# Perceiver block on one core: cross attention with its probabilities normalised before they are turned

## The chip, the cores and the metric

One Trainium2 chip, of which the program uses 1 core. The time is that of one execution on the device, in microseconds, as the median of several runs. The profile is one further execution of the same program, recorded by the hardware profiler, with a time and a span of its own. TensorE does the matrix products, VectorE and ScalarE the work on their results in PSUM, GpSimd elementwise work in SBUF; SyncE issues the loads.

## The reference, cut to what matters

The block is a cross attention, a differential attention over heads with its feed-forward, and a layer of experts. Only the first is touched:

```python
def _L0_xattn_ref(x_q, x_k, x_v, W_Q, b_Q, ...):     # x_q (8, 64, 512), x_k = x_v (8, 1601, 512)
    Q = (x_q @ W_Q + b_Q).reshape(B, L, H, dk).transpose(0, 2, 1, 3)    # H = 16, dk = 32
    K = (x_k @ W_K + b_K).reshape(B, S, H, dk).transpose(0, 2, 1, 3)
    V = (x_v @ W_V + b_V).reshape(B, S, H, dk).transpose(0, 2, 1, 3)
    scores = jnp.einsum('bhld,bhsd->bhls', Q, K) / jnp.sqrt(jnp.float32(dk))
    attn = jax.nn.softmax(scores, axis=-1)
    ctx = jnp.einsum('bhls,bhsd->bhld', attn, V)
    ...
x = x + _L0_xattn_ref(_layernorm(x, axis=-1), ctx_1024, ctx_1024, ...)
```

## The kernel before

Everything is float32. Where a product must be exact to float32, each operand is split into a high part in the format fp32r and the rest (`_hi`, `_lo`), and `mm3` (L62) makes three matmuls of a pair.

The cross attention (L233) runs over 8 batches and, in each, two halves h of the heads: 16 units. A unit has 8 heads; two heads share a 128-row tile (their 64 queries each), so there are 4 tiles p of probabilities `prob[:, p]`, 128 x 1601, in two pair groups g. The four engines each have their own written-out order, `unit(b, h, last)`, and meet by semaphores:

- TensorE (L446): seven `values` steps (two 128-row tiles of the context each, V into PSUM), with eight `scores` steps put behind them by `STEPS_BEHIND` (L294): steps 0 to 3 are group 0, 4 to 7 group 1. Then, for each g, seven `turn` steps (transpose of two column tiles of both probabilities of the group), each followed by parts of the keys of the next unit (`HALVES_AT`) and by `weigh` of the step before (probabilities times values). Behind turn 2 of each group stands `sums` (L395): two matmuls of `ones` with a diagonal of inverse row sums, which lay the inverses out along the free axis. `select` (L437) gathers the group's output.
- VectorE (L604): low parts of values, keys and turned probabilities; `scores` copies scores from PSUM to `prob` and takes their maxima; `sums(b, h, g)` (L574) is the reciprocal of two row sums; `output` (L594) multiplies the four blocks of a group with the laid-out inverses `rsb`.
- ScalarE (L516): high parts; `exponentials` (L492) of a whole 128 x 1601 tile in place, with its row sum, for p = 0, 1 behind values 3 and 4 and for p = 2, 3 behind turns 1 and 3 of group 0; `inverses` (L498) writes the diagonals; `sums` (L511) copies the result to `rsb`.
- GpSimd (L321): for each batch and each of 4 chunks of 402 columns of the turned context, the high part by a multiplication with ones (L331) and the low part by a subtraction (L334). For all but the first batch it first waits for TensorE to have finished with the old chunk.
- SyncE (L297): context chunks into two buffers `craw`, each load behind the `c_lo` of the chunk two before (L306), and the queries `qbd`, each behind the scores of a whole unit (L310). These stand in one queue.

In the unit of the trace that is used below (batch 3, h = 0), the values begin at 422.8 us and the first turn at 447.65 us. Inside a unit, the wait of a first turn is this:

```python
                if t == 0:
                    pe.wait_ge(exp_done, b * 8 + (4 * h + 2 * g + 2))
```

## Time and profile before

| | us |
|---|---|
| median of 3 runs (1821.58 to 1823.15) | 1822.5 |
| profiled execution, its time | 1819.43 |
| its span | 1817.6 |
| TensorE busy in the span (matmuls) | 1425.5 |
| VectorE, GpSimd, ScalarE busy | 958.4, 654.7, 612.2 |

About 1.8 us of the execution lie outside of the span. Busy time is summed over the whole program; the cross attention takes about 63 to 975 us of the span, its 16 units 56.14 us each from the second on (the last is shorter, as it has no keys to make). In timelines and in stretches, all times count from the start of the span, and a bracket at the end of a line is the idle time before it with what ended that.

### The profile page before, as it was taken

To read this page: it belongs to the slowest core of one execution; us is meant where nothing else is said; L and a number is where in the kernel's file an instruction comes from. 1 tells how busy PE (TensorE), PEld (TensorE's weight loads), DVE (VectorE), ACT (ScalarE), POOL (GpSimd) and SP (SyncE) were. 2 spreads that over 40 slices of the span, in tenths; PEclk is the share of its full clock that TensorE was granted. 3 is DMA by queue.
4 is the path that set the end of the run, shared out by engine and by line. 5 is a ranking of instruction groups with operands and counts; after the bars stand their busy time and mean duration, and the time that the engine had idled before them with its cause. 6 is when DMAs were issued, how large, how long until landed. Compare 5 with 4: busy or idle time off the path is not lost. (4 is left out here: it accounts for less than half of the span.)

```text
span 1817.6 us, 23549 instructions
## 1 busy us (share of the span) xinstructions
PE 1425.5 (78%) x8688; PEld 1217.8 (67%) x8688; DVE 958.4 (53%) x2159; ACT 612.2 (34%) x1230; POOL 654.7 (36%) x260
## 2 busy tenths in 40 slices
PE   3599999999999999999996630112389565999995
PEld 2599999999999999999995420001267453555552
DVE  7155545555555555555554598995601553444443
ACT  4144344443445434454434232112321201232231
POOL 4505023050220502205003599895652312344442
PEclk8799999999999999999998765555689686999997
DMA  3401002010020200201003000000500209999999
GB/s 140 167 7 61 25 1 79 7 62 24 1 79 7 79 7 1 80 7 43 1 1 117 35 0 0 0 1 0 191 1 0 99 1 361 336 333 337 342 331 304
DMA packets 42619, 166.70 MB, mean 92 GB/s; under 512 B 5792, under 2 KB 6304, under 8 KB 33952
## 3 DMA queue, kind: packets, MB, share of 16 engines
q1 hardware_dynamic: 32352, 141.32, 21.2%
q0 software_dynamic: 10176, 24.12, 5.3%
q8 instruction: 62, 1.02, 0.2%
q14 instruction: 29, 0.24, 0.0%
HBM read 144.98 MB, written 20.45 MB: 91 GB/s over the span
## 5 line engine op out<-in xcount | busy, mean ns | idle before, releaser
L331 POOL TENSOR_TENSOR c_hi<-craw,ones 128x1608 fp32r<-128x1608 f32 x32 | 91.9, 2871 | 621.8 <-PE ps_x L66 548.1
L64 PE MATMUL ps_x<-wkv_hi,c_hi 128*128 128x256 f32 (+1 forms) x832 | 240.3, 289 | 0.0
L65 PE MATMUL ps_x<-wkv_lo,c_hi 128*128 128x256 f32 (+1 forms) x832 | 233.4, 281 | 0.0
L66 PE MATMUL ps_x<-wkv_hi,c_lo 128*128 128x256 f32 (+1 forms) x832 | 232.8, 280 | 0.0
L64 PE MATMUL ps_x<-c_hi,wkv_hi 128*128 128x402 f32 x512 | 196.2, 383 | 34.0 <-POOL c_lo L334 34.0
L583 DVE TENSOR_TENSOR pT<-ps_x,pT 128x512 fp32r<-128x512 f32 (+1 forms) x224 | 145.6, 651 | 125.9 <-ACT pT L508 122.7
L65 PE MATMUL ps_x<-c_lo,wkv_hi 128*128 128x402 f32 x512 | 178.0, 348 | 0.0
L66 PE MATMUL ps_x<-c_hi,wkv_lo 128*128 128x402 f32 x512 | 177.5, 347 | 0.0
L508 ACT CAST pT<-ps_x 128x512 fp32r<-128x512 f32 (+1 forms) x224 | 124.6, 557 | 140.2 <-PE ps_x L418 136.6
L553 DVE TENSOR_TENSOR vv<-ps_x,vv 128x512 fp32r<-128x512 f32 (+1 forms) x112 | 73.0, 652 | 176.7 <-ACT vv L489 176.7
L64 PEld LDWEIGHTS ps_x<-wkv_hi,c_hi 128*128 128x128 f32 (+1 forms) x832 | 153.2, 184 | 16.9 <-issue 16.9
L489 ACT CAST vv<-ps_x 128x512 fp32r<-128x512 f32 (+1 forms) x112 | 62.3, 556 | 288.1 <-PE ps_x L66 288.1
L1772 PE MATMUL ps_e<-e_w_gu,e_xT 128*128 128x512 f32 x344 | 157.5, 601 | 0.0
L547 DVE SCALAR_TENSOR_TENSOR kT_lo<-ps_x,bk,kT_hi 128x402 fp32r<-128x402 f32 x128 | 81.4, 636 | 140.8 <-ACT kT_hi L483 140.8
L65 PEld LDWEIGHTS ps_x<-wkv_lo,c_hi 128*128 128x128 f32 (+1 forms) x832 | 153.5, 184 | 0.0
L66 PEld LDWEIGHTS ps_x<-wkv_hi,c_lo 128*128 128x128 f32 (+1 forms) x832 | 153.3, 184 | 0.0
L1077 PE MATMUL ps_h<-ident,h_on 128*128 128x128 f32 x16 | 4.4, 432 | 178.8 <-POOL h_on L833 178.8
L433 PE MATMUL ps_x<-pT,vv 128*128 128x256 f32 (+1 forms) x832 | 135.1, 285 | 2.5 <-DVE pT L583 2.5
L566 DVE TENSOR_SCALAR_CACHE_REDUCE prob<-ps_x 128x402 f32<-128x402 f32 (+1 forms) x256 | 131.2, 569 | 0.0
L433 PEld LDWEIGHTS ps_x<-pT,vv 128*128 128x128 f32 (+1 forms) x832 | 124.8, 188 | 5.3 <-DVE pT L583 3.9
L418 PE MATMUL ps_x<-ident,prob 128*128 128x128 f32 (+1 forms) x832 | 127.0, 272 | 0.0
L1077 PEld LDWEIGHTS ps_h<-ident,h_on 128*128 128x128 f32 x16 | 2.9, 217 | 180.8 <-issue 99.0
(290 smaller groups left out, 3232.2 us busy)
## 6 DMA issues: line engine op xcount, KB each, us to landing
e_w_gu<-w_gu SPq DMA_DIRECT2D x49, 1024.0 KB, 8.1
craw<-ctxT SPq DMA_DIRECT2D x32, 804.0 KB, 4.5
e_w_dn<-w_dn SPq DMA_DIRECT2D x48, 512.0 KB, 5.6
f_raw<-slabs SPq DMA_DIRECT2D x8, 1024.0 KB, 4.8
h_raw<-slabs SPq DMA_DIRECT2D x5, 1024.0 KB, 4.9
qbd_dram<-qbd_all SPq DMA_DIRECT2D x2, 2048.0 KB, 6.9
qbd<-qbd_dram SPq DMA_DIRECT2D x16, 256.0 KB, 2.7
wraw<-w_qkv SPq DMA_DIRECT2D x3, 1024.0 KB, 8.4
```

The lines of the kernel that those rows point to most:

```text
L64: nc.tensor.matmul(out, a_hi, b_hi, start=start, stop=False)
L65: nc.tensor.matmul(out, a_hi, b_lo, start=False, stop=False)
L66: return nc.tensor.matmul(out, a_lo, b_hi, start=False, stop=stop)
L331: nc.gpsimd.tensor_tensor(c_hi[:, :, chunk(c)], craw[:, c % 2], ones[:, 0:1].unsqueeze(2).to_broadcast([P, KD, CW]), ALU.mult).then_inc(sp ...
L418: ins = nc.tensor.transpose(ps[0:r, 6 + n % 2, c:c + P], prob[:, 2 * g + j, P * st:P * st + r], ident[:])
L433: ins = nc.tensor.matmul(ps[:, 4 + g, 256 * j:256 * j + 256], vv[0:r, st, 2 * g + j].rearrange("p l c -> p (l c)"), pT[0:r, n % 2, st % 2, ...
L508: nc.scalar.copy(pT[0:r, n % 2, 0:w, :, 0].rearrange("p a j c -> p (a j) c"), ps[0:r, 6 + n % 2, 0:256 * w].rearrange("p (a c) -> p a c", ...
L547: nc.vector.scalar_tensor_tensor(kT_lo[:, m, chunk(c)], ps[:, n % KEY_BANKS, 0:CW], bk[:, 2 * h + m:2 * h + m + 1], f32(kT_hi[:, m, chunk( ...
L553: nc.vector.tensor_tensor(vv[0:r, 2 * v:2 * v + w, :, 1].rearrange("p a j c -> p (a j) c"), ps[0:r, V_BANK[v], 0:256 * w].rearrange("p (a ...
L566: ins = nc.vector.tensor_scalar(prob[:, p, CW * n:CW * n + w], ps[:, 2 * (i % 2) + j, 0:w], 0.0, None, ALU.add, ALU.max, accum_out=pmax[:, ...
L583: nc.vector.tensor_tensor(pT[0:r, n % 2, 0:w, :, 1].rearrange("p a j c -> p (a j) c"), ps[0:r, 6 + n % 2, 0:256 * w].rearrange("p (a c) -> ...
L1772: ins = nc.tensor.matmul(ps[:, GU], xT[:, b, P * g:P * g + P], w_gu[:, b, g], start=(g == 0), stop=(g == KD - 1))
```

## The change

The inverse of a row sum is applied by GpSimd to the whole tile `prob[:, p]` in SBUF, in place, before the tile is turned. The diagonals, the matmuls that lay them out, `rsb` and its copy are gone; `output` is a plain copy. The first turn of a group waits for both multiplications instead of both exponentials. VectorE takes the reciprocals one by one. The exponentials of p = 2, 3 stand one turn earlier. The high part of the context is made by ScalarE (`context`), put among the values of the units with h = 1, and GpSimd keeps the subtraction.

```diff
         def _(pool):
-            freed_by = (2, 4, 5, NV)
...
-                    pool.wait_ge(c_loaded[c % 2], b * 32 + 16 * (c // 2 + 1))
-                    nc.gpsimd.tensor_tensor(c_hi[:, :, chunk(c)], craw[:, c % 2], ones[...], ALU.mult).then_inc(split_hi, 1)
...
+            def split(b, c):
+                pool.wait_ge(split_hi, b * 4 + (c + 1))
+                nc.gpsimd.tensor_tensor(c_lo[:, :, chunk(c)], craw[:, c % 2], f32(c_hi[:, :, chunk(c)]),
+                                        ALU.subtract).then_inc(split_done, 1)
+
+            def normalise(b, h, p):
+                pool.wait_ge(inv_done, b * 8 + (4 * h + p + 1))
+                nc.gpsimd.tensor_scalar(prob[:, p, 0:S], prob[:, p, 0:S], rinv[:, p:p + 1], None, ALU.mult).then_inc(normed, 1)
...
         def _(pe):
             def scores(b, h, i):
-                elif i == 1:
-                    if b or h:
-                        pe.wait_ge(rsb_done, b * 4 + 2 * h)
...
-            def sums(b, h, g):
-                if g == 0:
-                    pe.wait_ge(sc_kept, b * 16 + (8 * h + 8))
-                else:
-                    pe.wait_ge(rsb_done, b * 4 + (2 * h + 1))
-                pe.wait_ge(diag_done, b * 8 + (4 * h + 2 * g + 2))
-                for j in range(2):
-                    ins = nc.tensor.matmul(ps[:, 3, ...], ones[:], diag[:, g, j], start=True, stop=True)
...
             def turn(b, h, g, t):
                 if t == 0:
-                    pe.wait_ge(exp_done, b * 8 + (4 * h + 2 * g + 2))
+                    pe.wait_ge(normed, b * 8 + (4 * h + 2 * g + 2))
...
         def _(act):
-            def inverses(b, h, g):
-                act.wait_ge(inv_done, b * 4 + (2 * h + g + 1))
-                for j in range(2):
-                    nc.scalar.activation(diag[:, g, j], ident[:], ACT.Copy, scale=rinv[...]).then_inc(diag_done, 1)
...
-            def sums(b, h, g):
-                act.wait_ge(sums_full, b * 4 + (2 * h + g + 1))
-                act.wait_ge(o_done, b * 4 + (2 * h + g + 1))
-                nc.scalar.copy(rsb[:, g], ps[:, 3, 256 * g:256 * g + 256]).then_inc(rsb_done, 1)
+            def context(b, c):
+                act.wait_ge(c_loaded[c % 2], b * 32 + 16 * (c // 2 + 1))
+                nc.scalar.copy(c_hi[:, :, chunk(c)], craw[:, c % 2]).then_inc(split_hi, 1)
...
             def unit(b, h, last):
                 for v in range(NV):
                     values(b, h, v)
+                    if h == 1 and not last and v in (2, 4, 6):
+                        context(b + 1, v // 2 - 1)
...
-                        if (g, t) in ((0, 1), (0, 3)):
+                        if (g, t) in ((0, 0), (0, 2)):
                             exponentials(b, h, 2 + t // 2)
+                        if h == 1 and not last and (g, t) == (0, 4):
+                            context(b + 1, 3)
...
         def _(dve):
             def output(b, h, g):
-                dve.wait_ge(rsb_done, b * 4 + (2 * h + g + 1))
-                    ins = nc.vector.tensor_tensor(oT[...], ps[q, 4 + g, own], rsb[q, g, c], ALU.mult)
+                    ins = nc.vector.tensor_copy(oT[...], ps[q, 4 + g, own])
...
             def unit(b, h, last):
                     for i in STEPS_BEHIND[v]:
                         scores(b, h, i)
-                sums(b, h, 0)
+                    if v in (4, 5):
+                        sums(b, h, v - 4)
```

Before the first batch, ScalarE makes chunks 0 and 1 at once, and chunks 2 and 3 behind the keys 1 and 3 of the first unit.

VectorE, second half of the values of the first unit, before. L553 is the low part of a values step, L566 the scores copied with their maxima, L571 the maximum of a group, L577 the reciprocal, L583 the low part of a turned tile:

```order
L553 TENSOR_TENSOR vv<-ps_x,vv 128x8x64 x2
L566 TENSOR_SCALAR prob,pmax<-ps_x 128x402 x4
L553 TENSOR_TENSOR vv<-ps_x,vv 128x8x64
L566 TENSOR_SCALAR prob,pmax<-ps_x 128x402 x2
L566 TENSOR_SCALAR prob,pmax<-ps_x 128x395 x2
L571 TENSOR_REDUCE nmax<-pmax 128x2
L553 TENSOR_TENSOR vv<-ps_x,vv 65x4x64
L577 RECIPROCAL rinv<-psums 128x2
L583 TENSOR_TENSOR pT<-ps_x,pT 128x4x128
```

The same place in the changed kernel:

```order
L541 TENSOR_TENSOR vv<-ps_x,vv 128x8x64 x2
L554 TENSOR_SCALAR prob,pmax<-ps_x 128x402 x4
L565 RECIPROCAL rinv<-psums 128x1
L541 TENSOR_TENSOR vv<-ps_x,vv 128x8x64
L554 TENSOR_SCALAR prob,pmax<-ps_x 128x402 x2
L554 TENSOR_SCALAR prob,pmax<-ps_x 128x395 x2
L559 TENSOR_REDUCE nmax<-pmax 128x2
L565 RECIPROCAL rinv<-psums 128x1
L541 TENSOR_TENSOR vv<-ps_x,vv 65x4x64
L571 TENSOR_TENSOR pT<-ps_x,pT 128x4x128
```

The reciprocal of the first tile now stands behind the scores 4 and 5, that of the second behind the scores 6 and 7 and the maximum of group 1, ahead of the last values step.

GpSimd in the cross attention of the changed kernel, from its start (batch 0) to the end of the multiplications of batch 1, h = 0; L323 is the low part of a context chunk, L328 the multiplication of a tile. Before, L331 and L334 alternated there, four times a batch:

```order
L323 TENSOR_TENSOR c_lo<-craw,c_hi 128x4x402 x4
L328 ISA
L328 TENSOR_SCALAR prob<-prob,rinv 128x1601 x4
L323 TENSOR_TENSOR c_lo<-craw,c_hi 128x4x402
L328 TENSOR_SCALAR prob<-prob,rinv 128x1601 x2
L323 TENSOR_TENSOR c_lo<-craw,c_hi 128x4x402 x2
L328 TENSOR_SCALAR prob<-prob,rinv 128x1601 x2
L323 TENSOR_TENSOR c_lo<-craw,c_hi 128x4x402
L328 TENSOR_SCALAR prob<-prob,rinv 128x1601 x4
```

In a unit with h = 0, the queue holds nothing but the four multiplications; in one with h = 1, the four subtractions for the next batch stand around them.

## Rows read from the trace of the kernel before

**Rows 1.** busy time by stretch (stretch, length, engines with counts, PEclk, DMA): one unit.

```profile
447.14:503.28 56.14, 56.14 (x424) 54.40 (x423) 29.63 (x76) 24.51 (x43) 12.45 (x4) 1.00 0.02 6
```

**Rows 2.** waits in the same unit (who waited for whom: us, times, longest).

```profile
POOL c_hi L331 <- PE ps_x L66: 80.0, 2, 78.7
```

**Rows 3.** timeline of TensorE around the row sums (start, us, what, count).

```profile
453.65 0.60 PE L418 MATMUL ps_x<-ident,prob 128*128 128x128 f32 x4
454.09 0.61 PE L403 MATMUL ps_x<-diag,ones 128*128 128x128 f32 x4
454.46 0.43 PE L64 MATMUL ps_x<-c_hi,wkv_hi 128*128 128x402 f32 x1
...
458.13 0.60 PE L418 MATMUL ps_x<-ident,prob 128*128 128x128 f32 x4
458.48 0.43 PE L64 MATMUL ps_x<-c_hi,wkv_hi 128*128 128x402 f32 x1
```

**Rows 4.** timeline of TensorE at the first turns of the pair groups.

```profile
447.65 0.60 PE L418 MATMUL ps_x<-ident,prob 128*128 128x128 f32 x4
...
463.95 0.60 PE L418 MATMUL ps_x<-ident,prob 128*128 128x128 f32 x4
```

**Rows 5.** timeline of VectorE, end of the unit's scores.

```profile
448.31 0.16 DVE L571 TENSOR_REDUCE nmax<-pmax 128x2 f32<-128x8 f32 x1
448.39 0.41 DVE L553 TENSOR_TENSOR vv<-ps_x,vv 65x256 fp32r<-65x256 f32 x1
448.72 0.15 DVE L577 RECIPROCAL rinv<-psums 128x2 f32<-128x2 f32 x1
```

**Rows 6.** GpSimd instructions by line, form (busy, mean ns | idle before).

```profile
L334 POOL TENSOR_TENSOR c_lo<-craw,c_hi 128x1608 fp32r<-128x1608 f32 x32 | 107.2, 3349 | 2.5
L331 POOL TENSOR_TENSOR c_hi<-craw,ones 128x1608 fp32r<-128x1608 f32 x32 | 91.9, 2871 | 621.8 <-PE ps_x L66 548.1 <-DMA craw<-ctxT 73.7
...
L1150 POOL TENSOR_TENSOR f_f_lo<-f_fT,f_f_hi 128x512 fp32r<-128x512 f32 x16 | 20.5, 1288 | 44.6 <-DVE f_f_hi L1193 44.6
...
L147 POOL MEMSET qbd_all<- 128x8192 f32 x1 | 6.9, 6924 | 0.3 <-POOLq L1898 0.3
...
L150 POOL TENSOR_TENSOR wq_lo<-wraw,wq_hi 128x2048 fp32r<-128x2048 f32 x1 | 4.5, 4487 | 4.0 <-ACT wq_hi L159 4.0
```

**Rows 7.** timeline of all engines, start of the cross attention and a batch change.

```profile
56.93 2.87 POOL L331 TENSOR_TENSOR c_hi<-craw,ones 128x1608 fp32r<-128x1608 f32 x1 [23.01 <-DMA craw<-ctxT]
...
63.22 0.70 PE L64 MATMUL ps_x<-c_hi,wkv_hi 128*128 128x402 f32 x1 [31.45 <-POOL c_lo L334]
...
81.93 0.45 PE L64 MATMUL ps_x<-c_hi,wkv_hi 128*128 128x402 f32 x1 [1.57 <-POOL c_lo L334]
...
507.26 2.87 POOL L331 TENSOR_TENSOR c_hi<-craw,ones 128x1608 fp32r<-128x1608 f32 x1 [6.94 <-DMA craw<-ctxT]
```

**Rows 8.** ScalarE's copy of 2048 columns within SBUF, all of the program.

```profile
L159 ACT CAST wq_hi<-wraw 128x2048 fp32r<-128x2048 f32 x1 | 1.9, 1897 | 7.6 <-DMA wraw<-w_qkv 7.6
```

**Rows 9.** busy time by stretch: after a wait, and after TensorE's last matmuls.

```profile
82.10:90.00 7.90, 7.90 (x54) 7.76 (x56) 1.27 (x2) 1.71 (x3) 0.00 (x0) 1.00 0.31 104
974.40:976.20 1.80, 0.00 (x0) 0.00 (x0) 0.88 (x4) 0.00 (x0) 0.00 (x0) 1.00 0.00 0
976.40:980.00 3.60, 0.00 (x0) 0.00 (x0) 2.74 (x4) 2.38 (x4) 0.00 (x0) 0.51 0.75 250
```

**Rows 10.** timeline of TensorE across a change of its clock.

```profile
1270.02 0.79 PE L64 MATMUL ps_h<-h_w_hi,h_a_hi 128*128 128x512 f32 x1 [1.40 <-DVE h_a_lo L979]
...
1272.75 0.63 PE L64 MATMUL ps_h<-h_w_hi,h_a_hi 128*128 128x512 f32 x1
1273.17 0.53 PE L65 MATMUL ps_h<-h_w_lo,h_a_hi 128*128 128x512 f32 x1
...
1274.01 0.40 PE L65 MATMUL ps_h<-h_w_lo,h_a_hi 128*128 128x512 f32 x1
1274.24 0.40 PE L66 MATMUL ps_h<-h_w_hi,h_a_lo 128*128 128x512 f32 x1
```

More of the change, by code:

```diff
@@ L321, in _ @@
         def _(pool):
-            freed_by = (2, 4, 5, NV)
-            def split(b, first):
-                for c in range(NCH):
-                    if not first:
-                        pool.wait_ge(v_full, b * (2 * NV) - (NV - freed_by[c]))
-                    pool.wait_ge(c_loaded[c % 2], b * 32 + 16 * (c // 2 + 1))
-                    nc.gpsimd.tensor_tensor(c_hi[:, :, chunk(c)], craw[:, c % 2], ones[:, 0:1].unsqueeze(2).to_broadcast([P, KD, CW]),
-                                            ALU.mult).then_inc(split_hi, 1)
-                    pool.wait_ge(split_hi, b * 4 + (c + 1))
-                    nc.gpsimd.tensor_tensor(c_lo[:, :, chunk(c)], craw[:, c % 2], f32(c_hi[:, :, chunk(c)]),
-                                            ALU.subtract).then_inc(split_done, 1)
-            for b in range(B):
-                split(b, b == 0)
+            def split(b, c):
[5 more added lines that the diff above has]
+                nc.gpsimd.tensor_scalar(prob[:, p, 0:S], prob[:, p, 0:S], rinv[:, p:p + 1], None, ALU.mult).then_inc(normed, 1)
+            for c in range(NCH):
+                split(0, c)
+            for b in range(B):
+                for p in range(4):
+                    normalise(b, 0, p)
+                if b < B - 1:
+                    split(b + 1, 0)
+                normalise(b, 1, 0)
+                normalise(b, 1, 1)
+                if b < B - 1:
+                    split(b + 1, 1)
+                    split(b + 1, 2)
+                normalise(b, 1, 2)
+                normalise(b, 1, 3)
+                if b < B - 1:
+                    split(b + 1, 3)
         @block.tensor
@@ L383, in scores @@
                     pe.wait_ge(qbd_loaded[h], b * 16 + 16)
[L384 to L387 removed]
+                elif i > 1:
                     pe.wait_ge(sc_kept, b * 16 + (8 * h + i - 1))
@@ L393, in scores @@
                         True, True).then_inc(sc_full, 1)
-            def sums(b, h, g):
-                if g == 0:
-                    pe.wait_ge(sc_kept, b * 16 + (8 * h + 8))
-                else:
-                    pe.wait_ge(rsb_done, b * 4 + (2 * h + 1))
-                pe.wait_ge(diag_done, b * 8 + (4 * h + 2 * g + 2))
-                for j in range(2):
-                    ins = nc.tensor.matmul(ps[:, 3, 256 * g + P * j:256 * g + P * j + P], ones[:], diag[:, g, j], start=True, stop=True)
-                ins.then_inc(sums_full, 1)
             def turn(b, h, g, t):
@@ L532, in unit @@
                                 keys(nb, nh, half // 2)
-                        if t == 3:
-                            sums(b, h, g)
+            context(0, 0)
+            context(0, 1)
             for n in range(8):
                 keys(0, 0, n)
+                if n in (1, 3):
+                    context(0, 2 + n // 2)
             for b in range(B):
@@ L572, in scores, with sums @@
                                             ).then_inc(max_done, 1)
-            def sums(b, h, g):
-                dve.wait_ge(exp_done, b * 8 + (4 * h + 2 * g + 2))
-                nc.vector.reciprocal(rinv[:, 2 * g:2 * g + 2], psums[:, 2 * g:2 * g + 2]).then_inc(inv_done, 1)
+            def sums(b, h, p):
+                dve.wait_ge(exp_done, b * 8 + (4 * h + p + 1))
+                nc.vector.reciprocal(rinv[:, p:p + 1], psums[:, p:p + 1]).then_inc(inv_done, 1)
             def turned(b, h, g, t):
@@ L598, in output @@
                     q = slice(32 * i, 32 * i + 32)
-                    c = slice(64 * i, 64 * i + 64)
                     own = slice(64 * (i % 2), 64 * (i % 2) + 64)
-                    ins = nc.vector.tensor_tensor(oT[q, 2 * h + g, bass.ds(b * L, L)], ps[q, 4 + g, own], rsb[q, g, c], ALU.mult)
+                    ins = nc.vector.tensor_copy(oT[q, 2 * h + g, bass.ds(b * L, L)], ps[q, 4 + g, own])
                 ins.then_inc(o_done, 1)
@@ L622, in unit @@
                                 keys(nb, nh, half // 2)
-                        if (g, t) == (0, 5):
-                            sums(b, h, 1)
+                        if (g, t) in ((0, 1), (0, 3)):
+                            sums(b, h, 2 + t // 2)
                         if (g, t) == (1, 1):
```

14 lines of the change are left out of this document (3 added, 11 removed).

## The prediction

> **What bounds the kernel now.** I looked first at the busy time by stretch. In one whole unit of the cross attention [rows 1], TensorE is busy for all 56.14 us of 56.14, at the full granted clock of 1.00; VectorE is at 29.6 us, ScalarE at 24.5, GpSimd at 12.5. The list of waits of the same stretch has no row of TensorE's matmuls at all; its longest is GpSimd's, 78.7 us for TensorE [rows 2], which is idle time that costs nothing. So these 16 units are bound by what TensorE is given to do. That has two sides: a matmul taken away comes off the end in full, and a wait that is given to TensorE is paid in full, since it has no idle time in which to absorb it. Last I read the timelines around the places that the change touches.
>
> **What is removed from TensorE.** Behind turn 2 of each group stand the four matmul records of L403. With them, 0.81 us pass from the start of the turn to the next key matmul (453.65 to 454.46), without them 0.35 (458.13 to 458.48) [rows 3]. So one place is worth 0.45 us, and there are 2 in each of 16 units: 32 x 0.45 = 14.4 us. In the last unit, which has no keys, part of it may be hidden; under 1 us, left out. ScalarE's diagonals and copies and VectorE's multiplication stood beside a full TensorE and are worth nothing. The wait of score step 1 shows no idle time before it either.
>
> **The start.** TensorE begins at 63.22, when the first `c_lo` is there; GpSimd began the high part at 56.93 and took 2.87 us for it [rows 7]. ScalarE copies 2048 columns in SBUF in 1.90 us [rows 8], so 1608 take about 1.5: the first keys begin 1.4 us sooner. Later GpSimd has only 3.35 us a chunk instead of 6.2 [rows 6], but ScalarE puts chunks 2 and 3 behind keys 1 and 3, so chunk 2 arrives at about 67.8 + 0.6 + 1.5 + 3.4 = 73.3 and chunk 3 at about 77.7, against 81.9 where TensorE waits last for one now [rows 7]. The whole start gains 4 us; bounds 2 and 5.
>
> **The wait that is added.** The first turn of a group waited for exponentials that had long been done. Now it waits for two GpSimd multiplications. In group 0, the first starts behind the scores 4 and 5 and is over in time. The second cannot start before the reciprocal of tile 1, and the order puts that on VectorE behind the scores 6 and 7 and the maximum of group 1. VectorE is at that maximum from 448.31, and the next instruction starts 0.08 us behind it, at 448.39 [rows 5]. A reciprocal there takes 0.15, so it is done at 448.54; with some 0.1 us to pass the signal, GpSimd starts at about 448.65. TensorE is at the turn at 447.65 [rows 4]. So it stands for 1.00 us before the multiplication has even started, then for its length X, then 0.05 us to be told: 1.05 + X. Behind the wait on its queue stand the keys of the next unit, which need nothing from it but can't pass.
>
> X isn't in the trace: GpSimd runs no multiplication of a tile by one value a row. Its nearest rows bound it [rows 6]. Two operands (`c_lo`, 1608 columns) take 3.35 us; a tensor and ones from one column (L331) 2.87; a memset of 8192 columns takes 6.92. From 512 and 2048 columns of the same subtraction (1.288 and 4.487 us) each column costs 2.08 ns and the fixed part is 0.22 us. Without it, L331 is 2.65 us / 1608 = 1.65 ns a column for two reads, the memset 0.82 ns for one write and no read. If a read and a write go side by side and two reads follow each other, as 1.65 = 2 x 0.82 suggests, one read costs 0.82 ns: X = 1601 x 0.82 + 220 = 1.53 us. Below, nothing but the memset's rate with no fixed part (1.31); above, 2.87 (as L331) or 3.35. I take 1.53, because the two rates fit. The stall is then 1.05 + 1.53 = 2.58 us, in each of 16 units: 41.3 us.
>
> The page "GPSIMD Engine Reference" of the Trainium skill (section 4.1) says that GpSimd is about half as fast as VectorE with two inputs and roughly at line rate with one; by that rule and its 1.2 GHz, 1601 columns would be an estimated 1.33 us, 3 us less in the sum. The trace bears out the first half (3.35 us for two inputs), and no row shows the second.
>
> **TensorE's clock.** A stall of 2.6 us is longer than any in the units now. After the wait of 1.57 us that ends at 81.93 the clock stays at 1.00 [rows 7, 9]. After the last matmuls of the cross attention, which are over by 974.4, it is still 1.00 until 976.2 and 0.51 from 976.4 [rows 9]: it went to the lower level (1.2 GHz) about 2 us into the idle time, after a last unit that was less dense. So 2.58 us lies beyond both, and I expect the lower level after some stalls; how many, no row says. What it costs: behind a wait at 1270.02, matmuls stand 0.42 us apart (1272.75 to 1273.17), and 0.23 once the clock is up, which is at 1273.2 [rows 10]. 3.2 us at 0.42 instead of 0.23 lose 1.5 us. I take it in two stalls of three: 16 x 2/3 x 1.5 = 16 us; bounds 0 and 24.
>
> **What is moved, at no cost.** Group 1: its second multiplication starts behind the reciprocal that VectorE makes after turned tile 3 and key 2. That key is complete on TensorE when turn 4 comes at 458.13 [rows 3]; ScalarE and VectorE take some 2 us for it, so the reciprocal is done 12.6 us after the first turn and the multiplication 14.2 us after it, and the turn of group 1 comes 16.3 - 0.45 = 15.9 us after it [rows 4]. That covers X up to 3.2 us. Units with h = 1: ScalarE now has four copies of 1.5 us for the next batch among its 24.5 us of work in 56. That of chunk 2 stands ahead of the first turned copy and waits for its load, which lands at 507.26 [rows 7], since its issue stands on SyncE's queue behind the queries and so behind the unit's scores. ScalarE is then free at 508.8. TensorE's first turn, 56.14 us behind that of rows 4, comes at 503.79, with the stall at 506.4. It needs the turned copies in the `weigh` just ahead of turn 2, which stands 6.0 us behind turn 0 (447.65 to 453.65 [rows 3, 4]); less 0.7 us for that `weigh` it comes at 511.7. They are ready at about 510.1. So 1.6 us are to spare, and what hides it is the keys. GpSimd's subtractions in h = 1 fall into its idle time (43 us of 56) and are at least 2 us ahead of their keys.
>
> **The sum.** -14.4 - 4 + 41.3 + 16 = +38.9 us. From the profiled execution, 1819.4, that is 1858.3; the median of the runs is 3.1 us above it, so 1861.
>
> **Rivals.**
> 1. The multiplication runs like the other GpSimd rows (2.4 to 3.35 us). For it: every elementwise row of the trace with a read costs at least 1.65 ns a column; against: the one-stream rate of the memset. With 2.87 the stall is 3.92, times 16 is 62.7, and the clock falls in all, 24: -18.4 + 86.7 = +68.3, 1891. Above 3.2 us, group 1 begins to wait too.
> 2. The clock holds. For it: it held at 1.57 us, and the units around are dense. Then -18.4 + 41.3 = +22.9: 1845.
> 3. The other side: the wait is hidden and the kernel gets faster. Mechanism: the wait at the first turn decides the sign from the point at which a stall costs more than 18.4 / 16 = 1.15 us a unit. It costs 1.05 + X, so the multiplication would have to take 0.1 us, or the reciprocal of tile 1 would have to come 2.5 us sooner than its place behind the scores 6 and 7. For it: that reciprocal's input, the exponential of tile 1, stands on ScalarE two values steps earlier. Against: VectorE takes its instructions in the order shown. It would give 1822.5 - 18.4 = 1804.
> 4. ScalarE, held by the load of chunk 2, becomes the chain in the 7 units with h = 1. It decides when the load lands more than 1.6 us later than now; at 3 us more, 7 x 1.4 = 10 us on top: 1871. For it: the copy does stand ahead of work for the unit; against: nothing in the change delays that load.
>
> **Numbers.** Forecast 50% (with its own range of 1850 to 1872), rival 1 27%, rival 2 14%, rival 3 4%, rival 4 5%. The range runs from the lower edge of rival 2 to the middle of rival 1: 1841 to 1893. 0.2% (3.6 us) is about what a measurement of this kernel can tell from no change. Faster takes only rival 3, 0.04; no change 0.02, for a stall of just 1.15 us; slower 0.94.
>
> **What would show it.** In the stretch of one unit, TensorE's busy time should go from 56.14 of 56.14 to about 55.2 of 57.8 (more of both where the clock is low); the list of waits should have TensorE's turn (L411 there) waiting for GpSimd (L328) 16 times, 2.6 us each, and nothing at the turn of group 1. The GpSimd row of the multiplication gives X: 1.3 to 1.7 for me, over 2.4 for rival 1. The granted clock of the units should be below 1.00 for me and stay there for rival 2. The first keys should start at 61.9. If TensorE doesn't wait at the first turn, the forecast is wrong in its main step; if it waits elsewhere, in its completeness.

## The result, and the profile after

| | before | after |
|---|---|---|
| median of 4 runs each | 1822.04 us (1821.10 to 1823.15) | 1926.46 us (1925.25 to 1927.89) |
| ratio to before, 95% interval | 1 | 1.0573 (1.0555 to 1.0591) |
| profiled execution, its span | 1817.6 | 1923.3 |
| first key matmul | 63.22 | 62.16 |
| first turn of unit 1 starts | 110.81 | 114.26 |
| one unit, first turn to first turn | 56.14 | 61.98 to 63.45, mean 62.65 |
| first turn of the last unit to the end of the stage | 21.39 | 25.80 |
| TensorE done with the cross attention ("end of the stage") | 974.30 | 1079.81 |
| from there to the end of the span | 843.3 | 843.5 |

The change is 5.7% slower; the forecast was 2.1%, and 1926 lies outside of the range that ended at 1893. All of the 105.5 us lie in the cross attention; what follows it is not touched and takes as long as before.

The units by stretch, a whole unit (first turn to first turn, batch 3), the part behind its wait, and all 15 (columns as in [rows 1]):

```profile
427.46:490.80 63.34, 58.04 (x414) 55.96 (x415) 29.87 (x77) 24.23 (x38) 27.09 (x7) 0.93 0.13 44
490.80:494.37 3.57, 3.57 (x13) 3.54 (x14) 0.69 (x1) 2.21 (x3) 0.00 (x0) 0.50 0.00 0
114.26:1054.01 939.75, 860.19 (x6210) 829.97 (x6211) 447.15 (x1155) 381.69 (x583) 352.96 (x88) 0.95 0.08 27
```

Before, TensorE was busy for all of the unit at a clock of 1.00 [rows 1]. Now it idles for 5.3 of 63.3 us, and for 3.57 us behind that it has half its clock. Its busy time rose from 56.14 to 58.04 although it has ten instructions fewer (424 to 414): they run slower. In a unit before, the list of waits had no row of TensorE [rows 2]. That of the whole program now has two that belong together, GpSimd's, which is its first, and TensorE's further down:

```profile
POOL prob L328 <- DVE rinv L565: 424.3, 47, 36.1
...
PE ps_x L411 <- POOL prob L328: 87.1, 17, 5.8
```

The first is GpSimd's idle time and costs nothing. The second is 16 first turns of group 0 (5.84 us in the first unit, 5.30 in each other) and one turn of group 1 in the last unit (1.68). The first unit waits longer because its first multiplication is not over when the reciprocal of tile 1 is there (109.78 against 109.15); in the others it just is. The timeline around one of the waits, TensorE, then VectorE, then GpSimd:

```profile
485.22 0.28 PE L66 MATMUL ps_x<-wkv_hi,c_lo 128*65 128x256 f32 x1
490.80 1.08 PE L411 MATMUL ps_x<-ident,prob 128*128 128x128 f32 x4 [5.30 <-POOL prob L328]
491.54 0.69 PE L64 MATMUL ps_x<-c_hi,wkv_hi 128*128 128x402 f32 x1
...
494.03 0.54 PE L65 MATMUL ps_x<-c_lo,wkv_hi 128*128 128x402 f32 x1
494.37 0.43 PE L66 MATMUL ps_x<-c_hi,wkv_lo 128*128 128x402 f32 x1
494.63 0.35 PE L64 MATMUL ps_x<-c_hi,wkv_hi 128*128 128x402 f32 x1
494.82 0.35 PE L65 MATMUL ps_x<-c_lo,wkv_hi 128*128 128x402 f32 x1
```

```profile
486.00 0.16 DVE L559 TENSOR_REDUCE nmax<-pmax 128x2 f32<-128x8 f32 x1
486.08 0.15 DVE L565 RECIPROCAL rinv<-psums 128x1 f32<-128x1 f32 x1
```

```profile
481.83 4.34 POOL L328 TENSOR_SCALAR prob<-prob,rinv 128x1601 f32<-128x1601 f32 x1 [32.83 <-DVE rinv L565]
486.32 4.33 POOL L328 TENSOR_SCALAR prob<-prob,rinv 128x1601 f32<-128x1601 f32 x1 [0.16 <-DVE rinv L565]
```

TensorE ends its values at 485.50. The reciprocal of tile 1 starts 0.08 us behind the start of the maximum, as forecast, and the multiplication starts at 486.32, 0.82 us after TensorE had run dry. It then takes 4.33 us and not 1.53. Matmuls behind the wait stand 0.34 us apart up to 494.37, and 0.19 from 494.63 on: up to there the clock is at its lower level (the row of 490.80 to 494.37 above has 0.50). The GpSimd group, to be read against [rows 6]:

```profile
L328 POOL TENSOR_SCALAR prob<-prob,rinv 128x1601 f32<-128x1601 f32 x64 | 277.2, 4336 | 424.3 <-DVE rinv L565 424.3
L323 POOL TENSOR_TENSOR c_lo<-craw,c_hi 128x1608 fp32r<-128x1608 f32 x32 | 106.7, 3346 | 225.7 <-ACT c_hi L498 225.7
```

The multiplication of a tensor by one value a row is slower than the subtraction of two tensors of the same size. The start went as forecast in its first step: ScalarE's copy takes 1.53 us, and the first keys come 1.06 us sooner, for a forecast of 1.4.

```profile
57.18 1.53 ACT L498 CAST c_hi<-craw 128x1608 fp32r<-128x1608 f32 x1 [20.60 <-DMA craw<-ctxT]
...
62.16 0.70 PE L64 MATMUL ps_x<-c_hi,wkv_hi 128*128 128x402 f32 x1 [30.65 <-POOL c_lo L323]
```

### The profile page after: what moved, and what is told of

The parts are those of the page before. It is cut to its first block and busy times, and to the rows that moved or that the text cites. A ratio compares the mean times of both kernels' runs of the same rounds, so it can differ in the third digit from the quotient of the medians.

```text
span 1923.3 us, 23171 instructions
## 1 busy us (share of the span) xinstructions
PE 1445.6 (75%) x8560; PEld 1233.7 (64%) x8560; DVE 961.9 (50%) x2191; ACT 630.3 (33%) x1166; POOL 839.4 (44%) x292
## 5 line engine op out<-in xcount | busy, mean ns | idle before, releaser
L328 POOL TENSOR_SCALAR prob<-prob,rinv 128x1601 f32<-128x1601 f32 x64 | 277.2, 4336 | 424.3 <-DVE rinv L565 424.3
L571 DVE TENSOR_TENSOR pT<-ps_x,pT 128x512 fp32r<-128x512 f32 (+1 forms) x224 | 145.8, 651 | 235.0 <-ACT pT L493 233.7
L64 PE MATMUL ps_x<-c_hi,wkv_hi 128*128 128x402 f32 x512 | 206.4, 403 | 31.7 <-POOL c_lo L323 31.7
L323 POOL TENSOR_TENSOR c_lo<-craw,c_hi 128x1608 fp32r<-128x1608 f32 x32 | 106.7, 3346 | 225.7 <-ACT c_hi L498 225.7
L411 PE MATMUL ps_x<-ident,prob 128*128 128x128 f32 (+1 forms) x832 | 138.6, 290 | 87.1 <-POOL prob L328 87.1
L65 PE MATMUL ps_x<-c_lo,wkv_hi 128*128 128x402 f32 x512 | 187.0, 365 | 0.0
L66 PE MATMUL ps_x<-c_hi,wkv_lo 128*128 128x402 f32 x512 | 185.5, 362 | 0.0
L411 PEld LDWEIGHTS ps_x<-ident,prob 128*128 128x128 f32 (+1 forms) x832 | 105.0, 149 | 91.9 <-issue 90.9
```

What stands on the lines that cost most here:

```text
L64: nc.tensor.matmul(out, a_hi, b_hi, start=start, stop=False)
L65: nc.tensor.matmul(out, a_hi, b_lo, start=False, stop=False)
L66: return nc.tensor.matmul(out, a_lo, b_hi, start=False, stop=stop)
L323: nc.gpsimd.tensor_tensor(c_lo[:, :, chunk(c)], craw[:, c % 2], f32(c_hi[:, :, chunk(c)]), ALU.subtract).then_inc(split_done, 1)
L328: nc.gpsimd.tensor_scalar(prob[:, p, 0:S], prob[:, p, 0:S], rinv[:, p:p + 1], None, ALU.mult).then_inc(normed, 1)
L411: ins = nc.tensor.transpose(ps[0:r, 6 + n % 2, c:c + P], prob[:, 2 * g + j, P * st:P * st + r], ident[:])
```

## The experiments

All but two change the kernel after; `e4_forms` and `e6_context` change the kernel before. The part behind the stage, which no run touches, took 842 to 847 us in most profiles and 856 in three (`e3_aside`, `e8_keys_first_bc`, `e11_scalar_start`); why is open. So small effects are read from the end of the stage, which is that of the one execution that was profiled. A period is the time from first turn to first turn.

| | time, us (runs) | TensorE's wait at the first turn | periods | end of the stage |
|---|---|---|---|---|
| before | 1822.0 | none | 56.14 | 974.3 |
| after | 1926.5 | 5.30 | mean 62.65 | 1079.8 |
| e1_half | 1899.8 (1) | 3.25 | 60.24, 60.24, then 61.4 | 1053.5 |
| e12_stall25 | 1852.6 (1) | 2.50 | 57.95, but 59.48 and 59.24 once each | 1004.4 |
| e2_eighth | 1836.2 (1) | 1.76 | 57.20 | 989.0 |
| e3_aside | 1829.7 (10) | none | 55.22 and 57.57, once 59.16 | 976.4 |
| e5_broadcast | 1891.4 (1) | 3.81 | 60.8, 60.8, 61.5, 59.25, repeated | 1045.7 |
| e6_context | 1829.4 (10) | none | 56.14 and 57.3 to 59.8 | 982.8 |
| e7_keys_first | 1896.6 (1) | 0.89 and 1.46; 5.3 in the last unit | not even | 1047.4 |
| e8_keys_first_bc | 1845.1 (4) | none but in the last unit | not even | 995.9 |
| e9_one_key_first | 1820.4 (10) | 0.59 and 2.12, first and last unit | not even | 973.5 |
| e10_scalar | 1809.8 (6) | none | 55.25 | 962.5 |
| e11_scalar_start | 1805.3 (7) | none | 55.25 | 957.3 |

**The length of the multiplication.** Only the first columns of a tile are multiplied: 800 of 1601, 200, and 500. The rest of the tile stays unnormalised. Nothing else changes, so this moves X and the wait alone.

```diff
-                nc.gpsimd.tensor_scalar(prob[:, p, 0:S], prob[:, p, 0:S], rinv[:, p:p + 1], None, ALU.mult)
+                nc.gpsimd.tensor_scalar(prob[:, p, 0:800], prob[:, p, 0:800], rinv[:, p:p + 1], None, ALU.mult)
```

> The changed kernel, but only the first 800 of 1601 columns of a tile are multiplied (the rest stays unnormalised). Theory: the loss is the wait at the first turn, 1.1 us plus the multiplication, and TensorE's clock behind it. At 4.34 us for 1601 columns, 800 take about 2.3 us, the wait is about 3.3 us instead of 5.3, and with the clock still falling behind each wait the time is about 1887 us. Rival 1, the clock doesn't fall behind a wait of 3.3 us: about 1860. Rival 2, the loss does not hang on this instruction (ScalarE's copies, or GpSimd disturbing others): within 15 us of 1926.

> The changed kernel, but only the first 200 columns of a tile are multiplied (the rest stays unnormalised). Theory: the multiplication takes about 0.7 us, the wait at the first turn about 1.7 us. A wait of 1.57 us left the clock up in the kernel before, so the clock stays up and the time is about 1822 - 17 + 16 x 1.8 = 1834 us. Rival 1, any wait at this place brings the clock down: about 1860. Rival 2, a fixed cost of the instruction rather than one a column: over 1890.

> The changed kernel, but only the first 500 columns of a tile are multiplied (the rest stays unnormalised), so that the wait at the first turn is as long as the prediction had it: 0.28 + 500 x 2.525 ns = 1.54 us of multiplication, a wait of 2.5 us. The prediction had the clock fall behind two of three such waits, for 1.5 us each. Theory: with that, periods of 55.2 + 2.65 + 1.0 = 58.9 us on average, some at 57.9 and some near 59.5. Rival 1, it falls behind all, as at 3.25 us: near 60. Rival 2, behind none, as at 1.75: all at 57.9.

Measured: one wait of each, of 800, 500 and 200 columns, in this order, each with the matmul behind it where it shows the clock.

```profile
477.53 1.09 PE L411 MATMUL ps_x<-ident,prob 128*128 128x128 f32 x4 [3.25 <-POOL prob L328]
...
479.08 0.54 PE L66 MATMUL ps_x<-c_hi,wkv_lo 128*128 128x402 f32 x1
```

```profile
402.58 0.63 PE L411 MATMUL ps_x<-ident,prob 128*128 128x128 f32 x4 [2.50 <-POOL prob L328]
402.96 0.43 PE L64 MATMUL ps_x<-c_hi,wkv_hi 128*128 128x402 f32 x1
```

```profile
451.86 0.63 PE L411 MATMUL ps_x<-ident,prob 128*128 128x128 f32 x4 [1.76 <-POOL prob L328]
452.24 0.43 PE L64 MATMUL ps_x<-c_hi,wkv_hi 128*128 128x402 f32 x1
```

The multiplication takes 2.29, 1.54 and 0.78 us for 800, 500 and 200 columns, and the wait is 0.96 to 0.98 more each time. So what stands beside the multiplication is settled: about 1 us, as forecast, and the wait follows X one to one. The other thing that these three show is the clock. In the 15 units that have a full unit behind the wait it never fell behind 1.76 us, fell behind 2 of the 15 waits of 2.50 us, and behind all of 3.25. Without a fall a wait costs 0.23 us beside itself (57.20 - 55.22 - 1.75, and 57.95 - 55.22 - 2.50, where 55.22 is the period without a wait, from the next experiment); a fall costs 1.3 to 1.5 more at 2.50, and 1.5 (two units) or 2.7 (the others) at 3.25 (60.24 and 61.44, less 55.22, 3.25 and 0.23). e2_eighth came near its expectation (1836.2 for 1834). e1_half did not: 1899.8 for 1887, since each wait cost 2.8 us beside itself, clock and restart together. e12_stall25, a single run, has nearly the wait that was forecast, and came out at 1852.6: so 1861 was 8 us too high even for that wait. Of its periods 13 of 15 are as the rival "behind none" had them.

**The wait taken away, the work left.** GpSimd writes its product to a buffer that nobody reads, and the turn waits for the exponentials as before; each multiplication still takes its turn on GpSimd. Two waits that guard the buffers, of GpSimd for its own last product and of VectorE's scores for the products of the unit before, come with it and are not shown below.

```diff
-                nc.gpsimd.tensor_scalar(prob[:, p, 0:S], prob[:, p, 0:S], rinv[:, p:p + 1], None, ALU.mult)
+                nc.gpsimd.tensor_scalar(aside[:], prob[:, p, 0:S], rinv[:, p:p + 1], None, ALU.mult)
...
-                    pe.wait_ge(normed, b * 8 + (4 * h + 2 * g + 2))
+                    pe.wait_ge(exp_done, b * 8 + (4 * h + 2 * g + 2))
```

> The changed kernel with the multiplication in full, but its result goes to a tile that nobody reads (probabilities are used unnormalised), and the first turn waits for the exponentials only. Theory: what is left is the gain, 32 pairs of row-sum matmuls at 0.45 us and 2.5 us of the start, so about 1805 us, with TensorE full in a unit of 55.2 us and its clock at 1.00. Rival: the multiplications and the copies disturb others (SBUF access, ScalarE held by the load of a chunk): over 1815.

Measured: ratio 1.0016 (0.9985 to 1.0047), 1829.7 us where about 1805 was expected. The period from an h = 0 unit's first turn on is 55.22, which prices the row sums at 56.14 - 55.22 = 0.92 us a unit (0.90 forecast), and no matmul slows down beside 64 long multiplications on GpSimd. So the loss is the wait and what it does to the clock. But the other periods are 57.57, and this is what the expectation missed. TensorE waits twice in them:

```profile
508.44 0.50 PE L425 MATMUL ps_x<-zero 128*128 128x512 f32 x1 [1.36 <-DVE pT L576]
510.31 0.45 PE L64 MATMUL ps_x<-c_hi,wkv_hi 128*128 128x402 f32 x1 [0.46 <-POOL c_lo L324]
```

The first is the first `weigh`, which waits for turned copies that stand behind the copy of chunk 2 on ScalarE; the second is a key matmul that needs a context chunk which GpSimd has late. That is the mechanism of rival 4 of the prediction, without a later load: the 1.6 us to spare were there only because the stall gave them. In one of the seven units (59.16) the clock fell too, behind waits of 0.78 and 1.05 us that stand 2.5 us apart.

**The form of the multiplication.** Single instructions put on GpSimd behind the first batch of the kernel before, 128 x 800 each (the second `tensor_scalar` 400).

```diff
+            nc.gpsimd.memset(fa, 1.0)
+            nc.gpsimd.tensor_scalar(fb, fa, one, None, ALU.mult)          # one = ones[:, 0:1]
+            nc.gpsimd.tensor_scalar(fb[:, 0:400], fa[:, 0:400], one, None, ALU.mult)
+            nc.gpsimd.tensor_scalar(fb, fa, 0.5, None, ALU.mult)
+            nc.gpsimd.tensor_copy(fb, fa)
+            nc.gpsimd.tensor_tensor(fb, fa, one.to_broadcast([P, 800]), ALU.mult)
+            nc.gpsimd.tensor_tensor(fa, fa, fb, ALU.mult)
```

> The kernel before, with single GpSimd instructions on 128x800 put into GpSimd's idle time behind the first batch's split: memset, multiplication by one value a row (800 and 400 columns), by a constant, copy, multiplication of a tensor by a repeated column, and of two tensors. It costs nothing, about 1822 us. Theory A (the value a row is what is slow): by a value 2.3 us at 800, by a constant and the copy under 1 us. Theory B (every one-input instruction of this kind is slow): all three at about 2.3. In both, the repeated column takes about 1.5 us and two tensors about 1.9, by L331's and L334's rates.

Measured, GpSimd's timeline (start, duration):

```profile
82.07 0.76 POOL L341 MEMSET probe<- 128x800 f32 x1
82.93 2.30 POOL L343 TENSOR_SCALAR probe<-probe,ones 128x800 f32<-128x800 f32 x1
85.33 1.29 POOL L345 TENSOR_SCALAR probe<-probe,ones 128x400 f32<-128x400 f32 x1
86.70 2.21 POOL L347 TENSOR_SCALAR probe<-probe 128x800 f32<-128x800 f32 x1
88.98 0.85 POOL L349 COPY probe<-probe 128x800 f32<-128x800 f32 x1
89.92 1.52 POOL L351 TENSOR_TENSOR probe<-probe,ones 128x800 f32<-128x800 f32 x1
91.52 1.92 POOL L353 TENSOR_TENSOR probe<-probe 128x800 f32<-128x800 f32 x1
```

The rate that I had worked out for one read exists: a copy takes 0.85 us. But `tensor_scalar` does not run at it. It takes (2.30 - 1.29) / 400 = 2.5 ns a column and 0.28 us fixed, which gives 4.32 for 1601 columns (4.34 found), and with a constant nearly as much (2.21). So the number of streams is not what prices it, and neither theory holds as a whole: the constant is as slow as the value a row, the copy is not. Each row here is a single instruction; the times of 64 instructions each in the three runs above lie on the same line. The same product written as `tensor_tensor` with a repeated column takes 1.52.

**The other form in the kernel.**

```diff
-                nc.gpsimd.tensor_scalar(prob[:, p, 0:S], prob[:, p, 0:S], rinv[:, p:p + 1], None, ALU.mult)
+                nc.gpsimd.tensor_tensor(prob[:, p, 0:S], prob[:, p, 0:S], rinv[:, p:p + 1].to_broadcast([P, S]), ALU.mult)
```

> The changed kernel, with the multiplication written as one of two tensors, the second being the inverse repeated along the columns (the form of L331). Theory: its form sets its price, 1.52 us at 800 columns, so about 2.9 at 1601 instead of 4.34. The wait becomes about 3.85 us, the unit's period 55.2 + 4.0 + about 2.3 of clock = 61.5 instead of 62.65, and the time about 1908 us. Rival (in this place any form takes 4.3): 1926.

Measured: 1891.4; the multiplication takes 2.853 us, the wait 3.81 in each of 16 units. The form of one instruction is worth 35 us. It came out 17 us better than expected, for the most part because the clock's falls cost less than behind 5.3 us: in 3 of 15 units (59.25) it did not fall, in the others a fall cost 1.5 to 2.3; the last unit is 2.7 us shorter as well. This is rival 1 of the prediction as it was worked out there (2.87 us, 1891). That the time agrees so closely is in part luck: rival 1 had the clock fall in all units at 1.5 us each, it fell in 12 of 15 and cost more where it fell.

**The context alone.** The kernel before, with the high part of the context on ScalarE, placed as in the kernel after.

```diff
+            def context(b, c):
+                act.wait_ge(c_loaded[c % 2], b * 32 + 16 * (c // 2 + 1))
+                nc.scalar.copy(c_hi[:, :, chunk(c)], craw[:, c % 2]).then_inc(split_hi, 1)
...
+                    if h == 1 and not last and v in (2, 4, 6):
+                        context(b + 1, v // 2 - 1)
```

> The kernel before with one part of the change alone: the high part of the context on ScalarE, at the same places. Theory: 2.8 us are gained at the start, but in the 7 units with h = 1 ScalarE stands for the load of chunk 2 ahead of the first turned copy, as in the run with the result put aside, where these units took 2.35 us more: 1822 - 3 + 16 = 1835 us, waits of TensorE for VectorE at the first weighing and for GpSimd at the keys of chunk 1. Rival (that cost came with the multiplications): 1819.

Measured: ratio 1.005 (1.0025 to 1.0075), 1829.4 where 1835 was expected: this half of the change by itself is slower. The start gains 4.25 us (first turn at 106.56), and seven h = 1 units lose 1.2 to 3.6 us each. ScalarE and TensorE in one of them:

```profile
508.72 1.54 ACT L512 CAST c_hi<-craw 128x1608 fp32r<-128x1608 f32 x1 [3.71 <-DMA craw<-ctxT]
```

```profile
511.52 0.51 PE L423 MATMUL ps_x<-zero 128*128 128x512 f32 x1 [1.62 <-DVE pT L589]
```

ScalarE idles 3.71 us for the load with turned tiles waiting behind it; so with no stall to hide it, rival 4's mechanism acts. The unit that lost 3.6 us shows one thing more. Its wait of 1.78 us stands alone, and the clock fell 1.1 us behind its end:

```profile
739.33 0.50 PE L423 MATMUL ps_x<-zero 128*128 128x512 f32 x1 [1.78 <-DVE pT L589]
```

```profile
740.50:743.80 3.30, 3.30 (x15) 3.27 (x13) 1.63 (x3) 2.19 (x4) 0.97 (x1) 0.50 0.38 105
```

So the clock also fell behind a wait as short as that in a full unit, although it fell behind none of the 15 of 1.76 us in e2_eighth.

**Keys ahead of the first turn.** Two keys (four halves) of the next unit stand before the first turn, to give TensorE work during the multiplications; the last two turns then have none beside them. Copies of chunks 1 and 2 move to fit. Once with each form of the multiplication.

```diff
-        HALVES_AT = [(0, 1), (2, 3)] + [(i,) for i in range(4, 16)]
+        HALVES_FIRST = (0, 1, 2, 3)
+        HALVES_AT = [(i,) for i in range(4, 16)] + [(), ()]
...
+                for half in () if last else HALVES_FIRST:
+                    keys(nb, nh, half // 2, half % 2, (b, h))
                 for g in range(2):
                     for t in range(NV):
```

> The changed kernel, output as the reference, with keys 0 and 1 of the next unit put ahead of the first turn on all engines (they need nothing of the probabilities), the other keys one half behind each turn; chunk 1 of the context is split ahead of the multiplications, and ScalarE's copy of chunk 2 stands behind turned copy 1. Theory: 4.4 us of keys cover the wait of 5.3, so about 1.0 us stays with h = 0 and 1.7 with h = 1, too short for the clock to fall; periods 56.2 to 57, only the last unit (no keys) waits in full: about 1827 us. Rival (the wait is not from the multiplication behind the reciprocal): near 1926.

> As the kernel with keys 0 and 1 ahead of the first turn, and the multiplication with a repeated column (about 2.9 us). Theory: 1.05 + 2.9 = 3.95 us lie under 4.4 us of keys, so TensorE waits nowhere but in the last unit, periods of 55.2 us in both halves: about 1822 - 14 - 3 + 6 = 1811 us, faster than both kernels. Rival (moving keys brings new waits behind the first turns, where weighing has less beside it): 1820 or more.

Measured: both expectations are missed, by some 70 and 34 us. With `tensor_scalar` the first turn's wait shrank to 0.89 in h = 0 units and 1.46 in h = 1, and the turn of group 1 in h = 1 units began to wait in its place, 3.09. With the other form these are gone, and the wait that stays is one behind the last turns of each unit, which the first form has too. Two turns of the one, then from the list of waits of the other (the 36.9 us are the start of the stage for the most part):

```profile
536.66 0.63 PE L412 MATMUL ps_x<-ident,prob 128*128 128x128 f32 x4 [1.46 <-POOL prob L329]
553.65 0.52 PE L412 MATMUL ps_x<-ident,prob 128*128 128x128 f32 x3 [3.09 <-POOL prob L329]
```

```profile
PE ps_x L64 <- POOL c_lo L324: 36.9, 9, 30.3
PE ps_x L427 <- DVE pT L578: 22.3, 19, 1.3
```

The 3.09 is the next group's turn, 17 us later: GpSimd has a subtraction of 3.35 us and two multiplications of 4.34 to do there, 12 us in all, and the second of their reciprocals comes in the midst of it; the subtraction itself had waited for ScalarE's copy of chunk 2. The 22.3 us are `weigh` steps that wait for turned copies: one of 1.32 us in each of 15 units (19.8), the rest in the last. They stand at the last two turns, which have no key beside them to cover ScalarE and VectorE. The keys that were moved had been the cover of the turns that they left.

**One key ahead, with the reciprocals early.** Halves 0 and 1 go ahead, each later turn keeps one half, the form is the repeated column, and both reciprocals stand behind values 4, ahead of the late scores.

```diff
+        HALVES_FIRST = (0, 1)
+        HALVES_AT = [(i,) for i in range(2, 16)]
...
-                    if v in (4, 5):
-                        sums(b, h, v - 4)
+                    if v == 4:
+                        sums(b, h, 0)
+                        sums(b, h, 1)
```

> The changed kernel, output as the reference, with the multiplication by a repeated column (2.85 us); the reciprocals of tiles 0 and 1 both stand behind the scores 4 and 5, key 0 stands ahead of the first turn and each of the 14 turns has one half key behind it; ScalarE's copy of chunk 2 behind turned copy 1; GpSimd's multiplication of tile 2 ahead of its split of chunk 2. Theory: the second multiplication ends 2.3 us behind the old place of the first turn, key 0 covers 2.2, and no turn is left without keys as in the kernel with two keys ahead: periods of 55.3 (h = 0) and up to 56.3 (h = 1), about 1814 us. Rival (GpSimd is too full in h = 1 and gives new waits at keys or at the turn of group 1): 1822 or more.

Measured: ratio 0.9978 (0.9957 to 1.0000), 1820.4 where 1814 was expected, stage over at 973.46. The first turns wait no more but in the first unit (0.59) and the last (2.12); one wait of 1.06 us is left, in group 1 of h = 1 units. So 106 us of loss are undone with the multiplication still on GpSimd, yet hardly anything is gained over before: two units take 112.28 us, where twice 56.14 is the same.

```profile
517.24 0.63 PE L413 MATMUL ps_x<-ident,prob 128*128 128x128 f32 x4 [1.06 <-POOL prob L329]
```

**The multiplication on ScalarE.** ScalarE normalises (tiles 0, 1 behind values 4, 5; tiles 2, 3 behind turned 3, 5 of group 0), the reciprocal of tile 0 stands ahead of the scores 4 and 5 and that of tile 1 behind them, and GpSimd makes both parts of the context as before. In `e11_scalar_start`, ScalarE also makes the high part for the first batch, in whose start it idles.

```diff
+            def normalise(b, h, p):
+                act.wait_ge(inv_done, b * 8 + (4 * h + p + 1))
+                nc.scalar.activation(prob[:, p, 0:S], prob[:, p, 0:S], ACT.Copy, scale=rinv[:, p:p + 1]).then_inc(normed, 1)
...
+                    if v in (4, 5):
+                        normalise(b, h, v - 4)
...
+                        if (g, t) in ((0, 3), (0, 5)):
+                            normalise(b, h, 2 + t // 4)
```

> The changed kernel, output as the reference, with the multiplication on ScalarE (a copy with a scale a row, 1.65 us as an exponential of this size), for tiles 0 and 1 behind the values 4 and 5, for 2 and 3 behind turned copies 3 and 5; the reciprocal of tile 0 ahead of the scores 4 and 5, that of tile 1 behind them; the context's high part on GpSimd as in the kernel before. Theory: tile 1 is ready 0.3 us before the first turn, nothing waits, periods of 55.2 us, about 1808 us. Rival (ScalarE's work between turned copies makes TensorE wait): periods of 56 or more, 1820 or more.

> As the one with the multiplication on ScalarE, and the high part of the first batch's context also on ScalarE, as in the changed kernel's start; later batches' on GpSimd. Theory: some 3 to 4 us less than that one, about 1804 us, faster than both kernels. Rival (the start's gain needs the changed order of later batches, or is lost): as that one.

Measured: ratios 0.9915 (0.9885 to 0.9944) and 0.9886 (0.9855 to 0.9916), 1809.8 and 1805.3 us where 1808 and 1804 were expected. ScalarE's group, and one unit of e11_scalar_start:

```profile
L489 ACT ACTIVATE prob<-prob,rinv 128x1601 f32<-128x1601 f32 x64 | 104.8, 1637 | 0.0
```

```profile
492.00:547.25 55.25, 55.25 (x416) 53.51 (x414) 29.68 (x78) 28.40 (x42) 12.42 (x4) 1.00 0.19 66
```

The same product takes 1.64 us on ScalarE, with no idle time before it, and TensorE is busy for 55.25 of 55.25 us again at the full clock: [rows 1] without the row sums. All periods are 55.25. e11_scalar_start beats both kernels: 1805.3 us, 1.1% under before. Its stage ends 17.0 us sooner; the execution that was profiled has the long remainder of 856.4 us and took 1815.5, the other six took 1801.8 to 1806.7. Both kernels also have the reciprocal of tile 1 earlier than the changed kernel has it; no run moves that reciprocal alone, so its share is open.

## Why the prediction was wrong

The 105.5 us by the steps of the prediction, from the trace:

| step | forecast | measured |
|---|---|---|
| row sums gone | -14.4 | -13.8 (15 periods x 0.92) |
| start | -4 | -2.4 (114.26 - 5.84 - 110.81) |
| waits at the first turn | +41.3 | +85.4 (5.84 + 15 x 5.30) |
| clock, with the restart | +16 | +31.9 (15 x (62.65 - 55.22 - 5.30)) |
| last unit | 0 | +4.4 (25.80 - 21.39) |
| sum | +38.9 | +105.5 |

- **Right:** that TensorE bounds the units, so that a wait is paid in full; which turn waits and for whom; that the reciprocal's place behind the maximum sets the start (5.30 - 4.33 = 0.97 us in all beside X, for 1.05; of these 0.82 lie ahead of the multiplication, and 0.15 behind it, for 0.05; the 1.00 ahead of it in the forecast was counted from the turn's own place, some 0.15 us before TensorE is done with the matmul ahead); the row sums' price; ScalarE's copy (1.5, found 1.53).
- **Right in what came, wrong in its size:** no wait at the turn of group 1 in a full unit. The prediction had the reciprocal of tile 3 done 12.6 us behind the first turn, and room for X up to 3.2 us; by that, X = 4.34 would have brought a wait of 1.1 us. In e2_eighth, where the clock held, that reciprocal starts 10.99 us behind the first turn (462.85 against 451.86) and the turn comes at 15.90 (467.76). The 4.91 us between the two are the same in the kernel after, and the multiplication fits in with 0.28 us to spare, in all of the 15 full units:

```profile
441.04 0.15 DVE L565 RECIPROCAL rinv<-psums 128x1 f32<-128x1 f32 x1
```

```profile
437.01 8.66 POOL L328 TENSOR_SCALAR prob<-prob,rinv 128x1601 f32<-128x1601 f32 x2 [3.11 <-DVE rinv L565]
445.95 0.60 PE L411 MATMUL ps_x<-ident,prob 128*128 128x128 f32 x4
```

- **Wrong, the step that failed:** "one read costs 0.82 ns: X = 1601 x 0.82 + 220 = 1.53 us". It measured 4.336, which is 45 us of the 67 by which the sum was short. I took the operation for a stream of one read. The rate of such a stream was right (copy: 0.85 us for 800 columns), the operation was not such a stream. Its row stood nowhere in the trace, and 4.34 lies above even the upper bound of 3.35. That bound was too low: I had taken it from a row of this stage, and the trace of the kernel before has costlier products of GpSimd in later stages, where an operand is repeated:

```profile
L765 POOL TENSOR_TENSOR h_prod<-h_att,h_v 128x2048 f32<-128x2048 f32 x11 | 59.3, 5406 | 0.6
L833 POOL TENSOR_TENSOR h_on<-h_o,h_rrms 128x512 f32<-128x512 f32 x4 | 8.0, 2009 | 12.0 <-DVE h_rrms L974 12.0
```

  With 0.22 us fixed, the first of them comes to an estimated 4.27 us at 1601 columns. What makes these rows dear no run shows; that they were there should have widened the range. Against the choice spoke what rival 1 had noted: every elementwise row with a read cost at least twice my rate. I followed a ratio of two rates and gave the row of the nearest kind (L331: a product, read from one tensor and a repeated value) a lesser chance. e5_broadcast shows that this row prices its own form exactly, 2.85 for 2.87. For the form that was built, it too would have been 1.5 us short.
- The page "GPSIMD Engine Reference" (section 4.1) of the Trainium skill says that GpSimd is roughly at line rate with one input. The copy is in line with it (0.85 us for 800 columns); the multiplication by a value a row is not (2.30, 2.7 times as long). The rule's other half, on two inputs, the prediction had called borne out from GpSimd's row alone. The kernel before has one product that both engines make, at the same time (L761, 128 x 2048): 5.20 us on GpSimd and 3.58 on VectorE, 1.5 times as long.
- **The clock:** the second term that was mis-sized. At the wait that I had forecast the falls would have cost under 3 us and not 16 (e12_stall25: 2 of 15), and at the real one they cost 1.9 us a unit and not 1.0. The 0.23 us by which a wait costs more than its length, 3.5 us in all, stood in no term. The price of a fall, 1.5 us, was near what short waits cost (1.3 to 1.5) and under that of long ones (up to 2.7); how often it falls at which wait couldn't be had from a trace without such waits in full units.
- **Not seen:** the last unit, which has no keys beside its turns. Group 1 waits there, and 1.68 us of its 4.4 are that wait. In e1_half and e5_broadcast, where group 1 does not wait, it is still 1.67 us longer than before (23.06); the last 1.1 us are open.
- **The start** gave 2.4 us and not 4. In the other runs with this start it gave 2.1 to 4.3 (first turn less its wait, against 110.81), so the forecast lies within that spread.
- Rival 3's point, that a stall of 1.15 us decides the sign, is borne out from both sides but not pinned down: e2_eighth with 1.76 us ends 14.7 us late, and e10_scalar, whose units have no wait, 11.8 us early. No run lies between. Rival 4's mechanism is real and was hidden by the stall, as forecast; it costs 2.35 us in six of the seven h = 1 units of e3_aside, where the stall is away. That none of this could be seen in the time of the kernel after is why two halves of the change had to be run apart.

With the measured X, and the clock at the upper bound of its term, the prediction's own sum gives -18.4 + 16 x 5.39 + 24 = +91.8, 1914; the rest is the clock beyond that bound, the last unit and the start.

## What to carry to other kernels

On the engine that bounds a stage, a wait costs its length and often the clock as well (here behind none of 15 waits of 1.76 us but once behind one of 1.78, behind 2 of 15 of 2.50, and behind all of 5.30), so look for the last instruction that the wait hangs on and time that one first. An operation without a row in the trace is not priced by a count of its streams, and its upper bound comes from the costliest row a column that the engine has anywhere in the trace. Even the nearest row would have been 1.5 us short here: if the answer decides the size or the sign of a change, the instruction is timed alone before the kernel is rebuilt around it. Elementwise work for a full kernel goes where its idle time is and where it is short: the same product took 4.34 us on GpSimd in one form, 2.85 in another, and 1.64 on ScalarE.

## What the runs showed of the hardware that was not expected

- GpSimd, float32, 128 x 800: memset 0.76 us, copy 0.85, product with a repeated column 1.52, product of two tensors 1.92, `tensor_scalar` with a constant 2.21, with a value a row 2.30. `tensor_scalar` reads one tensor and is slower than the product of two.
- TensorE's granted clock behind a wait in otherwise full units: held behind all 15 of 1.76 us (e2_eighth), fell behind 2 of 15 of 2.50 us, 12 of 15 of 3.81 us, and all of 3.25 and of 5.30 us. It also fell once behind a single wait of 1.78 us (e6_context) and once behind 0.78 and 1.05 us in short succession (e3_aside). That the clock held behind three waits of 3.81 and behind none of 3.25 shows that the length of the wait alone does not decide; the pattern in e5_broadcast repeats every four units. What else does is left open.
- 64 multiplications of GpSimd of 4.3 us each beside a full TensorE (e3_aside) left the period of the h = 0 units at 55.22 us, and 64 of ScalarE (e10_scalar) left all at 55.25. VectorE's low part of a turned tile took 690 ns beside them and 691 before. No contention showed in these.
- A wait costs TensorE 0.23 us beside its idle time where the clock holds. In the kernel before, without a wait, the first turn starts at 447.65, 0.15 us ahead of the modelled end of the matmul before it; a wait takes this overlap away, which would be the larger part of the 0.23; no run was made for it.
